# Seven jobs moved out of the loop over pairs of heads, with the edits around them

## The reference, cut to what matters

```
x += xattn(LN(x), ctx)       # stage 0, masked, one head      (L0_xattn)
x += linear attention + MLP  # stage 1                        (L0_attn)
x += gated ternary MLP       # stage 2, 1024 wide, 2 hidden   (L0_ffn)
x += xattn(LN(x), ctx)       # stage 3, one head              (L1_xattn)
x += small self-attention    # stage 4                        (L1_attn)
x += top-1 mixture, 8 experts  # stage 5                      (L1_ffn)
x += xattn(LN(x), ctx)       # stage 6, one head              (L2_xattn)
x += self-attention, 16 heads  # stage 7                      (L2_attn)
x += top-2 mixture + 2 shared experts  # stage 8              (L2_ffn)
x += xattn(LN(x), ctx), 16 heads, masked  # stage 9           (L3_xattn)
x += retention, stage 10;  x += attention + mixture, stage 11
```

```
scores = einsum('bhqd,bhkd->bhqk', q, k) / sqrt(16);  scores = where(mask, -inf, scores)
ctx_out = einsum('bhqk,bhkd->bhqd', softmax(scores), v)
```

## Time and profile before

| what | value |
|---|---|
| median of 3 runs | 1566.28 us |
| profiled execution, its own time | 1570.01 us |
| its span, first to last instruction | 1568.2 us |
| PE busy | 1505.9 us (96%) |
| DVE, ACT, POOL busy | 837.3, 637.8, 151.6 us |
| mean granted TensorE clock | 0.991 |

### The profile page before, as it was taken

How to read it: one execution, slowest core, us unless ns; L and a number is a source line. 1 busy time by engine, 2 the same in 40 slices (tenths; PEclk the granted TensorE clock), 3 DMA queues, 4 the chain that set the end, 5 groups by cost and what they waited for, 6 DMA issues and landing times.

```text
span 1568.2 us, 24355 instructions
## 1 busy us (share of the span) xinstructions
PE 1505.9 (96%) x9939; PEld 960.6 (61%) x9950; DVE 837.3 (53%) x1488; ACT 637.8 (41%) x1208; POOL 151.6 (10%) x191
## 2 busy tenths in 40 slices
PE   8999999999999999999999999999999999998898
PEld 3667656886668745567655545555555454645697
DVE  4652645633332432432362368888988882566522
ACT  1312332221432422432352247777777675314122
POOL 0000330000000112000102042111000000100000
PEclk9999999999999999999999999999999999999999
DMA  9134141221023501022225167455658313210140
GB/s 375 52 107 173 61 139 50 81 89 41 0 99 114 180 20 46 0 81 79 99 71 183 26 166 119 78 88 92 163 113 181 51 17 138 86 54 1 38 178 14
DMA packets 40406, 146.87 MB, mean 94 GB/s; under 512 B 6092, under 2 KB 21708, under 8 KB 30668
## 3 DMA queue, kind: packets, MB, share of 16 engines
q1 hardware_dynamic: 40296, 145.32, 32.3%
HBM read 122.73 MB, written 22.56 MB: 93 GB/s over the span
## 4 chain that ended last, share of the span: by engine, by line
PE 87%; DVE 8%; ACT 3%; issue 1%; DMA 0%; SPq 0%; DVEq 0%; ACTq 0%
PE PS L162 55%; PE PS L2064 8%; PE PS L1976 7%; PE PS L1961 5%; PE PS L591 3%; PE PS L1398 2%; DVE SM L2080 1%; PE PS L1586 1%; PE PS L1409 1%; PE PS L2593 1%; PE PS L1599 1%; DVE CN L2644 1%; PE PS L2055 1%; PE PS L1606 1%; PE PS L2526 1%
## 5 line engine op out<-in xcount | busy, mean ns | idle before, releaser
L2080 DVE TENSOR_REDUCE SM<-PS 128x1 f32<-128x1024 f32 x256 | 302.4, 1220 | 50.9 <-PE PS L1961 49.5
L162 PE MATMUL PS<-CT,HT 128*128 128x512 f32 x416 | 190.4, 593 | 2.2 <-ACT HT L697 2.2
L162 PE MATMUL PS<-CN,AR 128*128 128x256 f32 (+1 forms) x832 | 188.0, 371 | 0.0
L162 PEld LDWEIGHTS PS<-CN,AR 128*128 128x128 f32 x832 | 151.0, 190 | 44.0 <-issue 28.7
L1976 PE MATMUL PS<-AR 49*128 49x256 bf16 (+1 forms) x1216 | 162.3, 271 | 3.0 <-issue 1.8
L162 PE MATMUL PS<-HT,AR 128*128 128x512 f32 x328 | 148.4, 601 | 2.3 <-ACT HT L346 1.3
L1976 PE MATMUL PS<-AR,CT 49*128 49x256 bf16 (+1 forms) x832 | 125.5, 274 | 0.0
L162 PE MATMUL PS<-AR 128*128 128x256 f32 (+3 forms) x504 | 114.9, 383 | 5.6 <-DVE AR L626 2.5
L648 DVE TENSOR_REDUCE SM<-AR 128x1 f32<-128x512 f32 x96 | 65.7, 686 | 100.8 <-ACT AR L701 99.1
L162 PEld LDWEIGHTS PS<-CT,HT 128*128 128x128 f32 x416 | 73.6, 190 | 71.1 <-issue 69.1
L162 PEld LDWEIGHTS PS<-HT,AR 128*128 128x128 f32 x328 | 60.4, 191 | 83.9 <-issue 80.7
(11 more groups left out here) (339 smaller groups left out, 2139.1 us busy)
## 6 DMA issues: line engine op xcount, KB each, us to landing
CN<-ctx_n SPq DMA_DIRECT2D x24, 1024.0 KB, 4.8
AR<-k_parts SPq DMA_DIRECT2D x114, 128.0 KB
CT<-pack SPq DMA_DIRECT2D x7, 2048.0 KB, 8.3
k_parts<-CN SPq DMA_DIRECT2D x32, 384.0 KB, 3.4
AR<-pack SPq DMA_DIRECT2D x20, 512.0 KB, 4.7
CT<-k_parts SPq DMA_DIRECT2D x78, 128.0 KB
CN<-v_ones SPq DMA_DIRECT2D x8, 1152.0 KB, 8.6
CT<-ctx_t SPq DMA_DIRECT2D x8, 1024.0 KB, 19.0
```

The lines of the kernel that those rows point to most:

```text
L162: last = te.matmul(o, l, r, start=first and k == 0, stop=final and k == n - 1, skip_group_check=True)
L2080: ve.tensor_reduce(MX9[:, p % 2, e, g % 8 // 4, g % 4:g % 4 + 1], PS[:, b:b + 2, :].rearrange("p a b -> p (a b)"), AX, ALU.max).then_inc(* ...
```

## The change

Places and numbers of jobs change, three helpers' calls are added, and the `heads` place goes from 11 k jobs to 4 (g = 1, 9, 17, 25). Stage 1 has two jobs more, stages 2, 3, 5, 6 and 8 one more each. The number of jobs in stages 4, 7 and 9's opening stays, but the kinds differ (in the opening, a k job stands where a v job stood). A new kind of place, `h1` to `h8`, holds one v job in two halves, each with its own PSUM bank, its own product of 256 columns (4 rows of the trace) and its own ACT copy.

```diff
-        for place, kinds in (("b1", "kvkv"), ("t1", "k"), ("s1a", "v"), ("s1b", "vv"), ("s1c", "v"), ("t1b", "k"),
-                             ("b2", "kv"), ("t2", "v"), ("b3", "kv"), ("t3", "v"), ("b4", "kv"), ("t4", "v"),
-                             ("b5", "kvk"), ("t5", "v"), ("b6", "kvkv"), ("t6", "k"), ("b7", "kvk"), ("t7", "v"),
-                             ("s7", "v"), ("b8", "kvkv"), ("t8", "k"), ("r8", "v"), ("b9", "vvk"), ("t9", "k"),
-                             ("s9", "kvvkvvvvvv"), ("heads", "k" * 11)):
+        for place, kinds in (("b1", "kvkv"), ("t1", "k"), ("s1a", "vv"), ("s1b", "vv"), ("s1c", "v"), ("h1", "v"),
+                             ("t1b", "k"), ("b2", "kv"), ("t2", "k"), ("s2", "v"), ("b3", "kk"), ("t3", "k"),
+                             ("h3", "v"), ("b4", "kv"), ("t4", "k"), ("b5", "kvk"), ("t5", "v"), ("h5", "v"),
+                             ("b6", "kkkk"), ("t6", "k"), ("h6", "v"), ("b7", "kvk"), ("t7", "v"),
+                             ("s7", "v"), ("b8", "kvkv"), ("t8", "k"), ("r8", "v"), ("h8", "v"), ("b9", "vvk"),
+                             ("t9", "k"), ("s9", "kvvkvvvkvv"), ("heads", "k" * 4)):
...
+        def half_pe(pe, place, y):
+            n = JOBS[place][0][1]
+            b, before = PB.take(("half", n, y), ("job", "v", n) if y else ("half", n))
+            pe.wait_ge(*before, ("w", 9))
+            mm(pe.e, PS[:, b, 0:256], [(CT[:, kt, (2 * n + y) * 128:(2 * n + y) * 128 + 128], Wv9[:, kt, :])
+                                       for kt in range(2)]).then_inc(
+                *(pe.inc("keys", "job_ps", "v", n) if y else pe.inc("keys", "half_ps", n)))
+        def half_act(ac, place, y):
+            n = JOBS[place][0][1]
...
+            ac.wait_ge(("job_ps", "v", n) if y else ("half_ps", n), ("stored", "v", V_BEFORE[n]))
+            ac.e.copy(...)
...                                            # xattn (stages 3 and 6), PE
+                if s:
+                    half_pe(pe, f"h{s}", 0)    # between q and the one-column product c
...
+                if s:
+                    half_pe(pe, f"h{s}", 1)    # between q2 and the first score chunk
...                                            # xattn, ACT: behind the t jobs, and behind the copies QN
+                    half_act(ac, f"h{s}", 0)
+                    half_act(ac, f"h{s}", 1)
...                                            # stage 1, PE and ACT
             jobs_pe(pe, "s1c")
+            half_pe(pe, "h1", 0)
...
+            half_pe(pe, "h1", 1)               # between the hidden products and the second MLP product
...                                            # stage 2: PE behind the up-projections, ACT behind warm(Gelu)
+            jobs_pe(pe, "s2")
+            jobs_act(ac, JOBS["s2"])
             jobs_pool(pl, "b2", *ht_all(2))
+            jobs_pool(pl, "t2")
+                if n == 2:
+                    jobs_sp(sp, "s2")          # SP, behind the first two loads of hidden weights
...                                            # stage 4, POOL
+            pl.end(4)
             jobs_pool(pl, "b4")
-            pl.end(4)
+            jobs_pool(pl, "t4")
...                                            # experts (stages 5 and 8), PE
                 rows8_pe(pe, s, R)
+                half_pe(pe, f"h{s}", 0)
...
+                half_pe(pe, f"h{s}", 1)
                 down(n - 1)
...                                            # experts, ACT
+                half_act(ac, f"h{s}", 0)
                 for e in range(n):
+                    if not gate_first:
+                        <wait for g_ps and the buffer, Silu of the gate>
                     if e < n_gated:
                         <wait for rb_ps, copy of the gate's row>
                     if gate_first:
                         <Silu in place>
-                    else:
-                        <wait for g_ps and the buffer, Silu of the gate>
+                half_act(ac, f"h{s}", 1)
...                                            # stage 9
-        for p in range(9):
-            for k in (1, 5) if p < 2 else (1,):
-                PAIR_JOBS[8 * p + k] = jobs.pop(0)
+        for p in range(4):
+            PAIR_JOBS[8 * p + 1] = jobs.pop(0)
```

More of the change, by code:

```diff
@@ L436, in job_act @@
                     *ac.inc("keys", "job", kind, n))
+        def half_pe(pe, place, y):
[7 more added lines that the diff above has]
+            n = JOBS[place][0][1]
+            v = VS9[V_SLOT[n]].rearrange("p (y c) -> p y c", y=2)[:, y, 0:272].rearrange("p (h r) -> p h r", r=17)
+            ac.wait_ge(("job_ps", "v", n) if y else ("half_ps", n), ("stored", "v", V_BEFORE[n]))
+            ac.e.copy(v[:, :, 0:16], bank("half", n, y)[:, 0:256].rearrange("p (h r) -> p h r", r=16)).then_inc(
+                *(ac.inc("keys", "job", "v", n) if y else ac.inc("keys", "half", n)))
         def jobs_act(ac, jobs):
@@ L761, in sync_1 @@
                 *sp.lands("mask_out", "mask_out"))
-            for place in ("b1", "t1", "s1a", "s1b", "s1c", "t1b"):
+            for place in ("b1", "t1", "s1a", "s1b", "s1c", "t1b", "h1"):
                 jobs_sp(sp, place)
@@ L911, in act_1 @@
             jobs_act(ac, JOBS["s1c"])
+            half_act(ac, "h1", 0)
             warm(ac, ACT.Gelu)
@@ L917, in act_1 @@
                     *ac.inc("gelu", "hd", 1, m))
+            half_act(ac, "h1", 1)
             end_act(ac, 1)
@@ L1215, in sync_3 @@
             jobs_sp(sp, "b3", "t3")
+            jobs_sp(sp, "h3")
             load_context(sp, 3, 1)
@@ L1444, in act_part @@
                 ae = ac.e
+                half_act(ac, f"h{s}", 0)
                 for e in range(n):
                     g, rb = GB[e % 2], RB[e % 2]
+                    if not gate_first:
+                        ac.wait_ge(("g_ps", s, e), gate_gone(e - 2) if e > 1 else None)
+                        ae.activation(g, bank("g", s, e), ACT.Silu).then_inc(*ac.inc("expert", "g", s, e))
                     if e < n_gated:
@@ L1452, in act_part @@
                         ae.activation(g, g, ACT.Silu).then_inc(*ac.inc("expert", "silu", s, e))
-                    else:
-                        ac.wait_ge(("g_ps", s, e), gate_gone(e - 2) if e > 1 else None)
-                        ae.activation(g, bank("g", s, e), ACT.Silu).then_inc(*ac.inc("expert", "g", s, e))
+                half_act(ac, f"h{s}", 1)
             return pe_part, dve_part, act_part
@@ L1506, in sync_5 @@
             jobs_sp(sp, "b5", "t5")
+            jobs_sp(sp, "h5")
         xattn_6 = xattn(6, W6, 4.0, (1810, 5906, 10002), False)
@@ L1513, in sync_6 @@
             jobs_sp(sp, "b6", "t6")
+            jobs_sp(sp, "h6")
             load_context(sp, 6, 1)
@@ L1853, in sync_8 @@
                     *sp.lands(f"v_in{q}", "v_in", 0, q))
+            jobs_sp(sp, "h8")
         sm_begin()
```

## The result

The changed kernel takes 1553.26 us, median of 4 runs (1549.74 to 1557.44), beside 1567.55 for the kernel before in 4 runs (1563.86 to 1569.54). The ratio is 0.9902, with a 95% interval of 0.9877 to 0.9927: 1.0% less time. The profiled execution took 1555.07 us with a span of 1553.2, against 1570.01 and 1568.2 before. Forecast were 1555.2 us and a sum of -11.1; the two profiled executions stand 14.9 apart, the medians 14.3. The time is in the range, but several terms behind it were off and cancelled, so that it came out this near is in part luck.

The account below looks back on a forecast made before the run. PE, busy 96% of the span with 87% of the chain, was taken as the bound. Terms -12.3 + 2.1 + 0.1 - 1.0 = -11.1 us took the median 1566.28 to 1555.2 us; 8 in 10 range 1549 to 1562.

Parts of the forecast that it names:

- The loop's jobs, -12.3: Stage 9 loop: seven k jobs leave, five at 1.82 us and two at 1.61, -12.3 us; bounds 11.3 to 13.4.
- The places, +2.1: Seven jobs moved into PE pauses of other stages cost only what exceeds the idle: +2.1 us, bounds 0 to 12.0.
- s1a ... Cost 0: Stage 1: one added v job fits PE's 1.72 us pause, which waits for DVE independently of the job; cost 0.
- rival B: Work moved is work paid: pauses' releasers come later through ACT's queue or the bank ring, 12.0 us return, 1566.0; chance 0.08.
- ACT, GpSimd and SP, 0: New places: copies, splits and stores stay covered, cost 0; moving stage 4's mark ahead of splits gives 0 to -0.64 us.
- Silu, +0.1: Stage 8: Silu ahead of the gate's row frees g1's bank in time; swap gives 0, bounds 0 to +0.6, +0.1 added.
- The clock, -1.0: Stages 3 and 6: half jobs fill idle ahead of the one-column product, avoiding half clock; 0 to -3.4 us, -1.0 taken.
- two chances of 3 in 10: Chance given to each of stages 3 and 6 that its clock fall, 1.7 us at half speed, goes.
- A: Instruction supply stalls job-free loop pairs, 5.45 us each; three make 1571.5; chance 0.04 for three or more, 0.08 for one or two.
- C: More than the jobs goes: both clock falls and pair 10's 5.45 us stall vanish, -19.0 us, 1547.3; chance 0.08.
- The signs: Forecast wrong if loop not 11 to 13 us shorter, "issue" idles over 2 us in pairs 4 to 8, or h pauses over 0.2.

Follow-up runs that it names:

- thin keys: Changed kernel with the key fetches from pair 3 or 4 on cut from 16 rows to one, so later pairs use stale keys: 1548.21 us.
- spread: Changed kernel plus separate banks for stage 1 and 7 jobs, a later GpSimd split, and half of each pair's key loads at step 4: 1549.51 us, ratio 0.9888.
- experiment on banks: Changed kernel with two stage 1 jobs given PSUM banks 6 and 7 and the stage 7 job bank 7, outside the ring: 1555.59 us.
- the fill: Kernel before, no job moved, with four 512-column bf16 products added in each of two pauses of stages 3 and 6: 1561.94 us, ratio 0.9958.
- the shift: Changed kernel with 64 one-column products ahead of the loop, moving later PE instructions on; no total given, loop stalls of 0.37, 1.78 and 1.68 us.
- thin jobs: Kernel before with the products of seven loop jobs cut from 512 columns to one, copies, splits and stores kept: 1559.35 us, ratio 0.9941.

## Why the prediction was right, and where it was not

1. **The loop's jobs, -12.3: right.** Measured 12.3 with the same two prices (1.60 and 1.82 in the stretches; five stretches of 21.84 in a row stand in the two kernels with no stall among them, thin keys and spread). The stretches of the loop gave the price; the distance of starts (1.91) would have given 13.4.

2. **The places, +2.1: too small by half.** Measured +4.2 without clock falls: stage 1 1.60, stage 2 0.53, stages 3 and 6 together about 0.04, stage 5 0.33, stage 7 0.84, stage 8 0.83. Of this, 0.24 in stage 5 belongs to point 3, so the places alone cost 3.9. The step that failed is "s1a ... Cost 0" and the silence on s7. I looked at who ends PE's pause and at its length, and not at which bank the added job takes from the ring. Each job or half job more ahead shifts every later user of the ring by a bank, and the ring runs on from stage to stage: with the change, six stages take more banks than before (1, 2, 3, 5, 6 and 8; the prediction says five), and ten more are taken ahead of stage 7. In stage 1 the v jobs behind then wait for DVE's division to free theirs (2 x 0.58), and in stage 7 the first score products wait for ACT's copy of a job that has always stood there (0.77). I named the ring for stage 8 and under rival B, but did not follow it in the others. The experiment on banks gives 1.54 and 0.84 of this back (and costs 0.6 in stage 11, by the same ring). The other places came out as costed: h8 0.83 for 0.86, s2 0.53 for 0.81, h3 and h6 less than the 0.22.

3. **ACT, GpSimd and SP, 0: right in the sum, wrong in how.** DVE's wait for GpSimd is gone, as forecast. But the norm's rows are 2.13 us longer beside the split, of which 0.24 reach the stage. Two engines with no semaphore between them were taken as independent. In stage 6 and for stage 2's loads no wait appeared.

4. **Silu, +0.1: right for the pair of edits (0 measured).** What fell short is the bound: without the swap it is 1.2 us and a clock fall of 1.7, not 0.6, because the gate's Silu stands behind two steps, the row's product and its copy.

5. **The clock, -1.0: too small.** In the profiled execution -3.4 for stages 3 and 6, so the two chances of 3 in 10 should have been near 1; the reason that I gave against ("the one-column product itself stays") is refuted by the fill. Over the timed runs the clock accounts for 14.0 - 7.4 = 6.6 us, or 5.5 on the one chip that had both; 3.4 of it are these two stages, and where the rest comes from is open. Without the time lost to the clock the kernel before takes 1555.0 us on average and the changed one 1546.0: -9.0, on the one chip -9.8. The terms that move no clock (-12.3 + 4.2 - 0.9) give -9.0, if the idles of the loop are on average as long as before.

6. **Rivals.** A: its mechanism is real, two of the five stretches that lost a job have stalls, of 0.71 and 3.03 us, but none of 5.45, and those of the earlier trace rows went in exchange; on the whole 5.5 us against 8.5. By the shift it is a matter of position; whether pairs without a job are also more exposed was not tested alone. B is refuted: 4.2 of 12.0 came back. C was right on both clock falls and half right on the stall.

7. **The signs.** No idle marked "issue" passed 2 us in pairs 4 to 8 (the longest is 1.72), and none of PE's pauses at the h places is left. But the loop is 16.3 us shorter, not 11 to 13, so by its own sign the forecast failed there: it had no term for the last but one stretch (0.9) and none for stalls that shrink (3.0).

The profiled executions' difference in full: -11.1 forecast, +2.1 more for the places and the split, -0.1 for Silu, -2.4 more clock in stages 3 and 6, -3.0 of stalls, -0.9 in the last but one stretch, -2.8 in stage 0, +1.7 for stage 8's fall and +1.6 behind stage 11 make -14.9. A step undersized by 2.1 was covered by others of the opposite sign. Left open: the last but one stretch is 0.94 us shorter in every kernel with the change and not in the one with thin jobs, so it comes from the moves and not from the missing columns. PE's waits for DVE L2101 and ACT L2150 there, 0.7 and 0.8 us in the kernel before, are 0.2 and 0.3 now. The loop's jobs took banks of the loop's own ring of three, and the thin jobs still do; that seven fewer takes shift its users is the candidate, and was not tried. That the stalls are equal on average in timed runs is inferred from the sums, since only profiled runs show them.

## What to carry to other kernels

When work is added to a pause, follow the ring of banks from there to the end of the program: each later user gets its neighbour's bank, and waits for whoever empties that. Here stages 7 and 11 paid for moves made elsewhere. A pause of less than a microsecond ahead of a thin product can be worth more than its length, since the clock may fall behind it (0.84 us of idle, 1.7 us of clock in stages 3 and 6); price it by the window with the fall and not by the idle time. And read a gain of one or two microseconds from its stage, since clock falls and supply stalls move a total by more.

## What the runs showed of the hardware

- DVE's four norm rows (128x256, SBUF to SBUF) took 1.38 us alone and 3.51 beside GpSimd's 128x512 operations, with no semaphore between them. The Trainium skill ("SBUF — State Buffer", "SBUF: two separate sides") says that GpSimd shares a pair of ports with those DVE operations that are in a two-port mode (or have two SBUF inputs), under an exclusive lock that one of them holds for a whole instruction. The rows agree with such a lock, though no row shows the mode: one by one the four operations took 0.41, 1.26, 0.75 and 1.33 us, against 0.41 each alone, and each of the last three ended 0.15 us behind the end of a GpSimd row (1.18, 0.61 and 1.17 us).
- The granted clock fell to 0.5, so from 2.4 to 1.2 GHz, for 3.4 us (6.8 in a few cases): behind 0.84 us of idle and a one-column product in stage 3, behind 1.18 us of idle in stage 8 with the old Silu order. A fall of 3.4 us cost 1.7 us in stages 3, 5, 6 and 8. In stage 0 it cost 1.7, or 2.8 to 3.0 when it came at 18.8 us or later; why is open. The same product with the idle filled by bfloat16 products kept 1.00.
- PE stood 1.72 us with nothing that the profile shows to wait for (1.4 to 2.7 in the other rows shown), while q1 took 98.8% of the DMA engines' time and q8 brought one 16 KB block. With thin key loads these idles were gone, and with 64 more products ahead two of the three stood in other stretches. In the spread kernel a window with a DMA share of 1.01 has PE busy 11.94 of 12 us: full queues alone do no harm. One block came in that window too, so what else decides is how soon PE needs it; that is inferred.
